# dt from eight sums per token and one stacked product, in place of three products with a folded weight

## The reference, cut to what matters

```python
h = rmsnorm(hidden, w_norm_in)
proj = h @ w_in_proj                       # [.., 1544]
...
dt_raw = proj[..., o4:]                    # the last 8 columns: one per head
...
dt = jax.nn.softplus(dt_raw @ w_dt + b_dt) # w_dt is [8, 256]
dt_h = dt.reshape(Bz, S, N_HEADS, HEAD_DIM).mean(-1)
```

## Time and profile before

| | |
|---|---|
| three runs | 564.02, 564.11, 567.18 us; median 564.11 |
| the profiled execution | 563.96 us, of which the span in the profile is 562.2 us |
| granted TensorE clock, mean | 0.998 |
| busy: PE, PEld, DVE, ACT, POOL | 541.9, 427.8, 443.7, 352.4, 173.6 us |
| matmuls | 3912 |

### The profile page before, as it was taken

How to read it: one execution, slowest core, us unless ns; L and a number is a source line. 1 busy time by engine, 2 the same in 40 slices (tenths; PEclk the granted TensorE clock), 3 DMA queues, 4 the chain that set the end, 5 groups by cost and what they waited for, 6 DMA issues and landing times.

```text
span 562.2 us, 11668 instructions
## 1 busy us (share of the span) xinstructions
PE 541.9 (96%) x3912; PEld 427.8 (76%) x3912; DVE 443.7 (79%) x1044; ACT 352.4 (63%) x760; POOL 173.6 (31%) x232
## 2 busy tenths in 40 slices
PE   8887989999999999999999999999999999999996
PEld 7666768878787777877787777778777787877774
DVE  4888878978889787878888788887888788775654
ACT  3884689547774578636776387745886377752442
POOL 3074016520162203620154201722055211532010
PEclk9999999999999999999999999999999999999999
DMA  6650036100560007200380005600162004400120
GB/s 202 186 144 22 1 91 163 59 1 2 159 170 1 2 6 225 101 1 0 117 189 21 0 0 175 151 0 0 41 209 76 0 0 143 169 2 1 33 67 19
DMA packets 37354, 41.41 MB, mean 74 GB/s; under 512 B 3483, under 2 KB 27717, under 8 KB 37317
## 3 DMA queue, kind: packets, MB, share of 16 engines
q1 hardware_dynamic: 36724, 40.80, 25.3%
q10 hardware_dynamic: 592, 0.15, 0.1%
HBM read 37.79 MB, written 3.15 MB: 73 GB/s over the span
## 4 chain that ended last, share of the span: by engine, by line
PE 60%; DVE 21%; ACT 8%; issue 7%; DMA 2%; POOL 2%; DVEq 0%; ACTq 0%; SPq 0%; POOLq 0%
PE bank L426 9%; PE bank L428 6%; PE bank L427 6%; PE bank L536 6%; PE bank L641 5%; PE bank L642 5%; PE bank L643 5%; DVE cv L1122 4%; DVE act_l L1273 4%; PE bank L548 3%; ACT act_h L873 3%; PE bank L564 2%; PE bank L522 2%; DVE dsum L1138 2%; PE bank L558 2%
## 5 line engine op out<-in xcount | busy, mean ns | idle before, releaser
L1273 DVE SCALAR_TENSOR_TENSOR act_l<-bank,act_h 128x512 fp32r<-128x512 f32 x192 | 131.6, 687 | 51.5 <-ACT act_h L873 49.4
L873 ACT ACTIVATE act_h<-bank 128x512 fp32r<-128x512 f32 x192 | 114.6, 597 | 84.9 <-PE bank L428 81.3
L1496 POOL TENSOR_TENSOR late<-late 128x512 f32<-128x512 f32 x31 | 39.8, 1285 | 167.2 <-DVE late L1281 166.7
L426 PE MATMUL bank<-fTl,w1h 128*128 128x512 f32 x192 | 87.1, 453 | 3.0 <-DVE act_l L1273 2.0
L893 ACT ACTIVATE seg<-seg,lneg 128x128 f32<-128x128 f32 x256 | 81.2, 393 | 1.5 <-DMA seg<-lc_rows 1.5
L641 PE MATMUL bank<-act_l,w2h 128*128 128x512 f32 x192 | 77.6, 404 | 1.5 <-DVE act_l L1273 1.5
L642 PE MATMUL bank<-act_h,w2l 128*128 128x512 f32 x192 | 76.0, 396 | 0.0
L428 PE MATMUL bank<-fTh,w1h 128*128 128x512 f32 x192 | 75.7, 394 | 0.0
L643 PE MATMUL bank<-act_h,w2h 128*128 128x512 f32 x192 | 75.5, 393 | 0.0
L427 PE MATMUL bank<-fTh,w1l 128*128 128x512 f32 x192 | 75.5, 393 | 0.0
L1483 POOL TENSOR_TENSOR xw<-xs,seg 128x128 f32<-128x128 f32 x48 | 20.2, 422 | 132.2 <-ACT seg L893 70.9
(11 more groups left out here) (177 smaller groups left out, 1058.9 us busy)
## 6 DMA issues: line engine op xcount, KB each, us to landing
seg<-lc_rows SPq DMA_DIRECT2D x32, 512.0 KB, 3.8
late<-gk_rows SPq DMA_DIRECT2D x8, 1024.0 KB, 8.8
grow<-lc_rows SPq DMA_DIRECT2D x48, 128.0 KB, 4.9
x_in<-L_attn_hidden_dram SPq DMA_DIRECT2D x8, 256.0 KB, 3.0
out_dram<-late SPq DMA_DIRECT2D x8, 256.0 KB, 5.3
late<-L_ffn_sw_dram SPq DMA_DIRECT2D x2, 512.0 KB, 6.4
late<-L_ffn_rw_dram SPq DMA_DIRECT2D x1, 1024.0 KB, 7.3
CT<-L_attn_w_in_proj_dram SPq DMA_DIRECT2D x1, 512.0 KB, 5.5
```

The costliest lines, as they stand in the source:

```text
L426: mm(dst, stat_h, mov_l, start=True, stop=False)
L873: nc.scalar.activation(act_h[:, b % RING, :], HID[b % 2][:], ACT.Relu).then_inc(act_h_ready, 1)
L1273: v_.scalar_tensor_tensor(act_l[:, r, :], HID[b % 2][:], 0.0, f(act_h[:, r, :]), ALU.max, ALU.subtract)\
```

## The change

The eight sums are made first and rounded there, and the folded weight is gone.

- `dt_sums(s)`: two matmuls of 512 columns into `TR` give, in rows 0 to 15, 32 to 47 and 64 to 79 alike, the eight sums by the high and by the low part of the eight weight columns (`wz_all` holds the three copies, `wz_high` their high parts alone).
- `z_copy(s)` on ScalarE writes all 128 rows to `zT`, rounded; `z_low(s)` on VectorE puts what is left after rounding into rows 32 to 47.
- `wdt` holds `w_dt` in the same rows: high, high, low. So one matmul of `zT` by `wdt` for each chunk is the sum of the three products, and `proj(s, 2)` and `proj(s, 3)` issue 4 matmuls of 256 columns, not 12.
- `dt_sums(s + 1)` stands in step 22 between `gram` and `proj(s + 1, 0)`, `z_copy(s + 1)` on ScalarE before `x_copy(s + 1, 0)`, `z_low(s + 1)` on VectorE before `act_low(18)`. `square_rows` now waits for `z_ready`, since it writes `TR`.
- In the opening the two matmuls L757 and L760, their copies and one wait are gone, as are five of the products that keep TensorE busy; `dt_sums(0)`, `z_copy(0)`, `z_low(0)`, the copy of `wdt` and its low part come in; x is projected before `dt`; six small transfers on SP in place of one on ScalarE's queue bring `w_dt`, each to eight rows of `wdt_raw`; GpSimd zeroes three more tiles.

```diff
@@ proj
-                if is_seq(s, 0) and j in (2, 6):
-                    pe.wait_ge(weights_set, 2 if j == 2 else 5)
+                if j in (2, 3):
+                    pe.wait_ge(z_ready, nth(s, 1, 1))
+                if is_seq(s, 0) and j == 2:
+                    pe.wait_ge(wdt_set, 2)
+                if is_seq(s, 0) and j in (0, 4, 6):
+                    pe.wait_ge(weights_set, (1, 2, 4)[j // 2 - (j > 0)])
...
                 elif j < 4:
                     for k in range(2):
                         c = 2 * (j - 2) + k
-                        ins = split(dst[:, k * DI:(k + 1) * DI], hTh[:, at(c)], hTl[:, at(c)], wh[:, DT0:DT0 + DI], wl[:, DT0:DT0 + DI])
+                        ins = mm(dst[:, k * DI:(k + 1) * DI], zT[:, at(c)], wdt[:], start=True, stop=True)
...
+            def dt_sums(s):
+                if is_seq(s, 0):
+                    pe.wait_ge(wz_set, 3)
+                pe.wait_ge(hTl_ready, nth(s, 1, 1))
+                mm(TR[:], wz_all[:], hTh[:], start=True, stop=False)
+                mm(TR[:], wz_high[:], hTl[:], start=False, stop=True).then_inc(z_psum, 1)
@@ square_rows
+                else:
+                    pe.wait_ge(z_ready, nth(s + 1, 1, 1))
@@ TensorE's scan_part
                         if c == NCH - 1 and not is_seq(s, n_seq - 1):
+                            dt_sums(s + 1)
                             proj(s + 1, 0)
@@ TensorE's opening
-                keep_busy_early(10)
-                pe.wait_ge(wdt_col_set, 1)
-                nc.tensor.transpose(MAIN[1][0:NH, 0:P], wdt_col[:], ident[:]).then_inc(wdtT_psum, 1)
-                pe.wait_ge(wdtT_set, 1)
-                pe.wait_ge(wdt_in, 16)
-                mm(MAIN[2][:, 0:DI], wdtT[:], w_dt[:], start=True, stop=True).then_inc(wdt_psum, 1)
-                keep_busy_early(8)
+                keep_busy_early(14)
...
-                keep_busy_early(5)
-                for j in (2, 3, 0, 1, 4, 5):
+                keep_busy_early(4)
+                dt_sums(0)
+                for j in range(6):
                     proj(0, j)
@@ ScalarE
+            def z_copy(s):
+                act.wait_ge(z_psum, nth(s, 1, 1))
+                nc.scalar.copy(zT[:], TR[:]).then_inc(z_high_ready, 1)
...
                         if c == NCH - 1 and not is_seq(s, n_seq - 1):
+                            z_copy(s + 1)
                             x_copy(s + 1, 0)
@@ VectorE
+            def z_low(s):
+                dve.wait_ge(z_high_ready, nth(s, 1, 1))
+                v_.tensor_tensor(zT[32:48, :], TR[32:48, :], f(zT[32:48, :]), ALU.subtract).then_inc(z_ready, 1)
...
+                    if s is not None and i == NBLK - 2 and not is_seq(s, n_seq - 1):
+                        z_low(s + 1)
                     if (new := block_at(i, prev, older)) and not (i == 0 and prev is not None):
                         act_low(*new)
@@ VectorE's opening
                 hT_low(0)
                 w_low(B0, 512, 512, 3)
+                z_low(0)
+                dve.wait_ge(wdt_set, 1)
+                v_.tensor_tensor(wdt[64:80, :], wdt_raw[64:80, :], f(wdt[64:80, :]), ALU.subtract).then_inc(wdt_set, 1)
                 w_low(C0, 1024, 512, 4)
```

More of the change, by code:

```diff
@@ L35 @@
 CLAMP = 30.0
-Z0, DT0, X0, B0, C0, WCOLS = 0, 256, 512, 768, 1280, 1792
+Z0, X0, B0, C0, WCOLS = 0, 256, 512, 1024, 1536
 def nth(s, per, k):
@@ L100, in build @@
         conv_w = sb("conv_w", [P, NB, TAPS])
-        w_dt = sb("w_dt", [NH, DI])
-        wdt_col = sb("wdt_col", [P, NH])
-        wdtT = sb("wdtT", [NH, P])
+        wz_all = sb("wz_all", [P, P], F32R)
+        wz_high = sb("wz_high", [P, P], F32R)
+        wdt_raw = sb("wdt_raw", [P, DI])
+        wdt = sb("wdt", [P, DI], F32R)
+        zT = sb("zT", [P, SEQ], F32R)
         b_dt = sb("b_dt", [P, DI])
@@ L199, in build @@
         zeros_set, tables_set = sem("zeros_set"), sem("tables_set")
[L200 to L201 removed]
+        cols_psum, cols_set, wz_set, wdt_set, z_psum, z_high_ready, z_ready = (sem(n) for n in ("cols_psum", "cols_set", "wz_set", "wdt_set", "z_psum", "z_high_ready", "z_ready"))
+        wh_set, weights_set = (sem(n) for n in ("wh_set", "weights_set"))
         a_exp_set, a_neg_set, b2_set, w_out_set = (sem(n) for n in ("a_exp_set", "a_neg_set", "b2_set", "w_out_set"))
@@ L294, in made @@
             if is_seq(s, 0):
-                return nth(s, 14, ((j + 2) % 4 if j < 4 else j) + 1)
+                return nth(s, 14, j + 1)
             return nth(s, 14, (25 - j if j > 11 else j) + 1)
@@ L333, in _ @@
                 r += v.shape[0]
+            sp_eng.wait_ge(zeros_set, 5)
+            for r in (0, 8, 32, 40, 64, 72):
+                sp_eng.dma_start(wdt_raw[r:r + NH, :], a["w_dt"]).then_inc(wdt_in, 16)
             sp_eng.dma_start(conv_w[:], a["conv_w"].rearrange("(b p) one k -> p b (one k)", p=P)).then_inc(conv_in, 16)
@@ L648, in fold_gate @@
                 pe.wait_ge(small_in, 3 * 16)
-                pe.wait_ge(hTl_ready, 1)
+                pe.wait_ge(z_ready, 1)
                 mm(TR[:, 0:NE], center[:], gw[:], start=True, stop=True).then_inc(gfold_psum, 1)
@@ L791, in opening @@
                     if c == NCH - 1:
+                        dt_sums(1)
                         proj(1, 0)
@@ L996, in opening @@
                 act.wait_ge(wcol_in, 16)
-                nc.scalar.activation(wdt_col[:], w_raw[:, 1536:1544], ACT.Identity, scale=wn_in[:]).then_inc(wdt_col_set, 1)
+                act.wait_ge(zeros_set, 7)
+                for t in (wz_all, wz_high):
+                    nc.scalar.activation(t[:, 0:96].rearrange("p (k q) -> p k q", q=32)[:, :, 0:NH],
+                                         w_raw[:, 1536:1544].unsqueeze(1).to_broadcast([P, 3, NH]), ACT.Identity, scale=wn_in[:]).then_inc(wz_set, 1)
                 act.wait_ge(wx_in, 16)
                 w_high(X0, 256, DI)
-                act.wait_ge(wdtT_psum, 1)
-                nc.scalar.copy(wdtT[:], MAIN[1][0:NH, 0:P]).then_inc(wdtT_set, 1)
                 act.wait_ge(wz_in, 16)
                 w_high(Z0, 0, DI)
-                act.wait_ge(wdt_psum, 1)
-                nc.scalar.copy(wh[:, DT0:DT0 + DI], MAIN[2][:, 0:DI]).then_inc(wdth_set, 1)
                 hT(0)
@@ L1008, in opening @@
                 w_high(B0, 512, 512)
+                z_copy(0)
+                act.wait_ge(wdt_in, 6 * 16)
+                nc.scalar.copy(wdt[:], wdt_raw[:]).then_inc(wdt_set, 1)
+                act.wait_ge(cols_psum, 1)
+                nc.scalar.mul(cols[:, 0:24], MAIN[3][:, 0:24], 1.0 / P).then_inc(cols_set, 1)
+                nc.scalar.copy(cols[:, 24:34], MAIN[3][:, 24:34]).then_inc(cols_set, 1)
                 w_high(C0, 1024, 512)
-                act.wait_ge(cols_psum, 1)
-                nc.scalar.mul(cols[:, 0:24], MAIN[0][:, 0:24], 1.0 / P).then_inc(cols_set, 1)
-                nc.scalar.copy(cols[:, 24:34], MAIN[0][:, 24:34]).then_inc(cols_set, 1)
                 act.wait_ge(alog_in, 16)
@@ L1373, in opening @@
                 dve.wait_ge(wn_in_in, 16)
+                dve.wait_ge(wz_set, 1)
+                high, low = (wz_all[:, 0:96].rearrange("p (k q) -> p k q", q=32)[:, :, r:r + NH] for r in (0, NH))
+                v_.scalar_tensor_tensor(low, w_raw[:, 1536:1544].unsqueeze(1).to_broadcast([P, 3, NH]), wn_in[:], f(high),
+                                        ALU.mult, ALU.subtract).then_inc(wz_set, 1)
                 norm1_apply(0)
                 w_low(X0, 256, DI, 1)
-                dve.wait_ge(wdth_set, 1)
-                v_.tensor_tensor(wl[:, DT0:DT0 + DI], MAIN[2][:, 0:DI], f(wh[:, DT0:DT0 + DI]), ALU.subtract).then_inc(weights_set, 1)
                 w_low(Z0, 0, DI, 2)
@@ L1407, in opening @@
                         hT_low(1)
+                    if i == NBLK - 2:
+                        z_low(1)
                 conv(1, 0, range(TAPS))
```

9 lines of the change are left out of this document (5 added, 4 removed).

## The result

| | median of the runs | span of the profiled execution |
|---|---|---|
| before | 564.39 us (11 runs, 563.92 to 567.18) | 562.2 us |
| after | 568.38 us (11 runs, 567.65 to 570.31, and one at 1790.07) | 565.9 us |

The ratio after to before is 1.007, 95% interval 1.0055 to 1.0086: the change makes the kernel 0.7% slower. 567.2 us was predicted. In the profiles the difference is 3.7 us.

What follows compares the result with a forecast made beforehand. The bound was taken to change along a sequence, with TensorE on the chain only in places. Six boundaries at 0.45 us (2.7) plus 0.4 from the opening gave +3.1 us, so 567.2 us; own range 565.7 to 569.2, 8-in-10 range 563.2 to 570.0.

Steps and rivals of the forecast that it cites:

- What bounds the kernel: Between sequences the chain of waits leaves TensorE from 243.27 to 254.97 us, block 18 to block 22, bypassing the dt products.
- Part 1: dt products cut from 12 to 4: 0.90 us of TensorE freed, turned into waiting at block 22, worth 0.
- TensorE is the bound after all: Rival: TensorE sets the pace, each sequence gains 0.45 us, 561.2 us with the opening; chance 0.12.
- Part 2: Two dt_sums products ahead of proj(s + 1, 0) and block 18 put 0.45 us on the path at each boundary.
- Absorbed: Rival: slack in VectorE's queue before block 18 hides the two products, only the opening counts, 564.5 us; chance 0.12.
- Parts 3 and 4: z_copy on ScalarE and z_low on VectorE fit into waiting time around block 18, z_low with 0.5 us spare: worth 0.
- Part 5: Sequence 0 to 1: dt ready 0.45 us sooner after its start, dt_sums(1) 0.45 us later, worth 0.
- Part 6: Opening: transposes 1.4 us sooner, then a new serial stretch to dt_add near 13.4 instead of 13.01: +0.4 us.

Runs made afterwards that it cites:

- e9: Kernel before with GpSimd's rstd ahead of the third term's sum, nothing else moved: 562.46 us, ratio 0.9968, period 64.75 us.
- e2: Kernel after with sums, copy and low part made for sequence 0 only, so later output is wrong: 565.98 us, ratio 1.0015, period 65.10 us.
- e1: Kernel before plus two unread 512-column products ahead of proj(s + 1, 0), twelve dt products kept: 568.31 us, ratio 1.006, period 65.53 us.
- e4: Kernel after with the sums moved ahead of block 19's second products, their copy and low part moved too: 567.05 us, ratio 1.0031, period 65.12 us.
- e6: Kernel after with VectorE's z_low made twice: 571.01 us, ratio 1.0107 to the kernel before, period 65.69 us.
- e3: Kernel after with the opening reordered: C's wh ahead of the dt copies, wdt's low part ahead of z_low: 568.97 us, ratio 1.0062.
- e7: Kernel before with GpSimd's rstd ahead of the third term's sum and VectorE's last convolution tap behind the mean square: 566.03 us, ratio 1.0024.
- e5: Kernel after run once more, unedited: 568.72 us, ratio 1.0082 to the kernel before, period 65.57 us.
- e11: Same kernel as e10 but with GpSimd's rstd back behind the third term's sum: 566.14 us, ratio 0.9994, period 65.10 us.
- e8: Kernel after with sums moved, opening reordered, and e7's early rstd and moved tap: 564.42 us, ratio 0.9994, period 64.75 or 65.35 us.
- e10: Same kernel as e8 without the moved tap, GpSimd's rstd still early: 563.90 us, ratio 0.997, period 64.77 us.

## Why the prediction was right

It held by its own steps. Two terms were too small: the opening by 0.35 us, and the six boundaries by some 0.4 in sum. That the whole still came within 0.6 us of the profiles' 3.7 is in part luck, as the end of this section shows.

- **What bounds the kernel.** Right: the chain leaves TensorE from block 18 to block 22. e9 shows it from the other side, since a shorter way there makes the period shorter.
- **Part 1, eight products worth 0.** Right, by e2 (65.10 against 65.07). The rival "TensorE is the bound after all" falls. The Trainium skill (Perfetto Trace Analysis, section "Identifying the Most-Contended Engine"), which the prediction drew on for this rival, asks to judge TensorE's headroom by MFU (the share of its peak rate that the products make) and the busy share of its weight loads, not by the 96% of its matmuls; weight loads were busy 76% here, under VectorE's 79%, so it speaks for the rival less than the prediction says. Whatever the share, 3.4 us less of TensorE's busy time came with 3.7 us more span.
- **Part 2, 0.45 us per boundary.** Right in place, a little small: 0.47 from the starts, 0.52 in the period. e1 gives 0.46 of it to the products. Followed along VectorE's `late`, the kernel after was 0.55 us behind the kernel before ahead of the first of the six boundaries (111.37 against 110.82) and 1.03 behind it (120.02 against 118.99). Each of the other five added 0.47 or 0.48 too, and another 0.02 to 0.07 came in each body between them, whose cause is open; the end was 3.62 behind. So the six gave 3.07 against 2.7. "Absorbed" falls with it, by e1 and by e4.
- **Parts 3 and 4, `z_copy` and `z_low` worth 0.** Right: `z_low` started at once after `mg`, with 0.52 us left over against the 0.5 forecast, and e6 found that room.
- **Part 5, sequence 0 to 1 worth 0.** Near: `dt_add` was 0.75 us late in the opening and 0.74 at sequence 1 (63.24 against 62.50). But from there to `fTl` VectorE took 2.26 us where it had taken 2.43 (65.50 against 64.93, now 0.57 late): 2.43 to 2.48 in the four profiles with twelve `dt` products, 2.25 or 2.26 in the nine with four. So the part was worth -0.2, and this is the one place where the saving showed.
- **Part 6, the opening.** The term was mis-sized: +0.4 forecast, +0.75 measured. The lead of 1.4 us at `hTh` was right, and so was ScalarE's end of C's `wh` (12.8 forecast, 12.85). The step that went wrong is the last one, VectorE's low part of C and `dt_add` "near 13.4". 12.8 and 0.7 are 13.5, so 0.1 was lost in the adding. VectorE's own queue was left out: `z_low` (0.68) and `wdt`'s low part (0.42) stand ahead of `wl` there and end at 12.95, so `wl` began at 12.98, 0.13 behind C's `wh`. And from its start to `dt_add` were 0.78, not 0.7. With the 0.05 of C's `wh` that makes the 0.36. The two ways to `wl`, by ScalarE and by VectorE's queue, end within 0.1 us of each other, which is why e3 had to shorten both to give back 0.39.

The sum is 0.75 - 0.2 + 3.07 = 3.6 us, and 3.1 was forecast; the spans differ by 3.7, the medians by 4.0. Two smaller slips: the range's lower end is worked from 563.96 and its upper end from 564.1, and the prediction said that a measurement tells 1% from no change, where the interval measured is 0.3% wide and tells the 0.7%.

The 0.75 holds for the two profiles compared, and the experiments showed that the opening of the kernel before has no one length. Its code is the same in four profiles, and `dt_add` started at 12.14 (e9), 12.24 (e1), 13.01 (before) and 15.12 us (e7). The new opening gave 13.76, 13.82, 13.83 and 13.84 (after, e5, e2, e4). TensorE's timeline of the opening shows where that comes from, in e7 and then in e9:

```profile
8.48 3.60 PE L437 MATMUL bank<-ident 128*128 128x128 f32 x16
```

```profile
7.04 2.05 PE L437 MATMUL bank<-ident 128*128 128x128 f32 x16
```

The same sixteen products took 3.60 us in one execution and 2.05 in the other, and started 1.44 us apart. The transposes of `hn` stand behind them, at 11.91 and 8.93. The pace is TensorE's clock. In each profile the products from 2.1 us on start 0.213 us apart and, from one moment on, 0.112: 1.2 and 2.4 GHz. The trace's record of the granted clock begins at that moment too, at 1.00; the views print 1.00 ahead of it as well, though there is no record there. It begins at 4.96 us in e9, 5.16 in e1, 6.76 in the kernel before and 11.75 in e7, in the order of the four starts of `dt_add`. TensorE had begun the same products at 2.13 or 2.14 us in all four; why the clock rose at different moments no run shows.

In the nine profiles of the new opening the clock rose between 5.19 and 7.36 us, and the transposes started at 7.87 to 7.94, as soon as `hn` was complete. TensorE had waited for it by up to 0.92 us (e5, rise at 5.19), and not at all at the two latest rises (7.17 in e6, 7.36 in e11). So a rise as late as e7's should delay the new opening as well; no profile shows one.

My +0.4 was reckoned from one draw of a number that ranges over 3 us, and its upper bound, worked from that draw, says nothing of the others: against e9's opening the new one is 1.6 us later, against e7's 1.4 us sooner.

## What to carry to other kernels

The value of an edit is decided by where the chain of waits runs at that moment: the same two products cost 0.47 us ahead of block 18 and 0.05 ahead of block 19's second products, and 0.9 us saved on an engine at 96% gave nothing. When work moves into an idle time, look at what ends that time; and when the chain is on a small operation of a slow engine, look at what stands ahead of it in its own queue: two GpSimd instructions exchanged gave 0.32 us per sequence. Judge such edits by the period between repeats, which tells 0.1 us, and not by the total alone; the first part of the kernel here moved by up to 3 us with the moment at which TensorE's clock rose, and by 1.2 to 1.55 us with a fall of it.

## What the runs showed of the hardware beyond this

- A GpSimd operation on 128x4 elements took 1.02 us alone and 1.46 to 1.58 us with a VectorE operation of 128x512 (two inputs in SBUF) beside it, in e7 at all six boundaries with the tap, in e8 at two of six. In e8 it is one or the other: where `rstd` took 1.58 us the tap took 0.75, and where `rstd` took 1.02 the tap took 0.78 or 0.79. That looks as if the one that comes second waits for the first, but the starts differ by 0.05 us in both cases, and no run shows what decides.
- VectorE took 0.68 us for 16 partitions and 512 columns, as for 128 partitions.
- TensorE's first products ran at 1.2 GHz (0.213 us from start to start) and changed to 2.4 GHz (0.112 us) at 4.96 to 11.75 us, from execution to execution.
- In seven of the thirteen profiles (e1, e2, e3, e6, e8, e9, e10) the granted clock fell to 0.50 for 3.41 us, from a start between 45.92 and 48.13 us, in the other six not. TensorE had two waits of about 0.75 us from 43.8 us on in all thirteen, so these alone do not explain it. In e3 `gram` took 2.08 us there in place of 1.16. From the third `mg` (near 44.6 us) to the first `rstd` were 12.32 us in e9 where they were 10.77 in the kernel before, and 12.34 in e10 where they were 11.14 in e11: the fall cost 1.55 and 1.2 us.
